# LayerNorm's normalization moved from VectorE to ScalarE in a three-part transformer stack

## The reference

```
def _layernorm(x, axis=-1, eps=1e-05):
    m = jnp.mean(x, axis=axis, keepdims=True)
    v = jnp.var(x, axis=axis, keepdims=True)
    return (x - m) / jnp.sqrt(v + eps)
...
    x = x + 0.5 * _L0_ffn_ref(_layernorm(x, axis=-1), ...)
    x = x + _L0_attn_ref(_layernorm(x, axis=-1), ...)
    x = x + 0.5 * _L0_ffn_ref(_layernorm(x, axis=-1), ...)
    x = x + 0.5 * _L1_ffn_ref(_layernorm(x, axis=-1), ...)
    x = x + _L1_attn_ref(_layernorm(x, axis=-1), ...)
    x = x + 0.5 * _L1_ffn_ref(_layernorm(x, axis=-1), ...)
```

## Time and profile before

| | |
|---|---|
| time, median of 3 runs | 4531.28 us (4527.89 to 4532.78) |
| the profiled execution | 4530.06 us |
| its span, first to last instruction | 4528.2 us |
| PE busy | 3917.3 us (87%) |
| DVE busy | 3219.1 us (71%) |
| ACT busy | 2058.9 us (45%) |
| POOL busy | 1146.4 us (25%) |
| L203, the normalization, 192 instructions | 80.1 us of DVE |
| L214, the power, 48 instructions | 48.5 us of POOL |
| L235, the copy of the transposes, 48 instructions | 28.7 us of ACT |

### The profile page before, as it was taken

One profiled execution on the slowest core, in us unless ns is written; L12 is line 12 of the kernel. 1 busy time (PEld: TensorE's weight loads), 2 busy tenths in 40 slices (PEclk: granted clock), 3 DMA queues, 4 the chain that ended last, 5 costly groups with the idle time before them and its releaser, 6 DMA issues. The chain is left out here.

```text
span 4528.2 us, 64140 instructions
## 1 busy us (share of the span) xinstructions
PE 3917.3 (87%) x23153; PEld 1796.6 (40%) x23153; DVE 3219.1 (71%) x6998; ACT 2058.9 (45%) x3088; POOL 1146.4 (25%) x943
## 2 busy tenths in 40 slices
PE   4799999968888849999999697758999999999865
PEld 2122222254444422222222544743444444444465
DVE  7799999926666678999997367665555555555565
ACT  3377777731145324777776311423333333333343
POOL 3000000000132130000000001753444444444465
PEclk9799999979999978999999798878999999999978
DMA  3111111120120031111111201430000000000144
GB/s 94 46 40 41 40 43 40 42 95 1 33 68 1 3 89 31 43 40 43 41 43 37 92 1 44 140 99 1 2 2 2 2 2 2 2 2 2 29 133 117
DMA packets 322709, 183.97 MB, mean 41 GB/s; under 512 B 169960, under 2 KB 282908, under 8 KB 322268
## 3 DMA queue, kind: packets, MB, share of 16 engines
q1 hardware_dynamic: 306044, 145.23, 11.8%
q0 software_dynamic: 14624, 34.37, 2.8%
q10 hardware_dynamic: 1728, 0.28, 0.0%
HBM read 109.91 MB, written 68.68 MB: 39 GB/s over the span
## 5 line engine op out<-in xcount | busy, mean ns | idle before, releaser
L646 DVE TENSOR_REDUCE ra_mh<-PS 128x1 f32<-128x512 f32 x2144 | 1341.9, 681 | 144.7 <-PE PS L524 135.8
L601 ACT ACTIVATE ra_p<-PS 128x1024 f32<-128x1024 f32 x1040 | 1011.8, 1021 | 482.3 <-PE PS L531 473.9
L524 PE MATMUL PS<-ra_k,ra_q 96*128 96x512 bf16 x2144 | 750.8, 392 | 2.3 <-DVE ra_mh L646 2.2
L540 PE MATMUL PS<-ra_p,ra_va 128*32 128x512 f32 x4192 | 569.2, 607 | 63.2 <-ACT ra_va L594 62.9
L531 PE MATMUL PS<-ra_q,ra_k 99*128 99x512 bf16 x2080 | 622.2, 380 | 1.7
L2081 ACT ACTIVATE ca_p<-PS 128x1024 f32<-128x1024 f32 (+3 forms) x384 | 310.8, 809 | 587.5 <-PE PS L2011 383.4
L2150 DVE TENSOR_REDUCE ca_mh<-PS 128x1 f32<-128x512 f32 (+3 forms) x768 | 388.1, 552 | 152.9 <-PE PS L1971 123.8
L500 POOL DMA_DIRECT2D o_heads<-ra_ot x134 | 70.3, 529 | 1649.3 <-ACT ra_ot L607 1649.3
L2116 POOL TENSOR_TENSOR ca_s<-ca_s,ca_p 128x1024 f32<-128x1024 f32 (+3 forms) x256 | 414.0, 1617 | 234.9 <-ACT ca_p L2081 229.6
L524 PEld LDWEIGHTS PS<-ra_k,ra_q 96*128 96x128 bf16 x2144 | 202.0, 97 | 659.8 <-DVE ra_mh L646 500.3
L2002 PE MATMUL PS<-ca_q,ca_k 64*128 64x512 f32 (+3 forms) x1536 | 344.4, 524 | 0.0
(11 more groups left out here) (270 smaller groups left out, 5616.8 us busy)
## 6 DMA issues: line engine op xcount, KB each, us to landing
ra_k<-qk_parts SPq DMA_DIRECT2D x136, 144.0 KB
ra_q<-qk_parts SPq DMA_DIRECT2D x408, 48.0 KB
o_heads<-ra_ot POOLq DMA_DIRECT2D x134, 128.0 KB, 3.4
ao_ot<-o_heads SPq DMA_DIRECT2D x16, 1024.0 KB
f_xg<-expert_tokens SPq DMA_DIRECT2D x56, 256.0 KB, 4.0
expert_outputs<-f_yb SPq DMA_DIRECT2D x56, 256.0 KB
qk_parts<-rp_parts SPq DMA_DIRECT2D x96, 128.0 KB, 2.4
expert_tokens<-X SPq DMA_DIRECT2D x28, 256.0 KB
```

What stands on the lines that cost most here:

```text
L524: pe.matmul(PS[:, 5 + place % 3, :], Q[0:KMAX, u, j, t * P:(t + 1) * P], K[0:KMAX, u, j, h * BT:(h + 1) * BT], start=True, stop=True).then ...
L540: mm = pe.matmul(PS[VW * j:VW * (j + 1), 4, :], VA[:, ub, step % KT, j, :], PR[:, s % 2, j, :], start=(s % KT == 0) if start is None else ...
L601: act.activation(PR[:, s % 2, PH * pair:PH * (pair + 1), :], PS[:, PH * pair:PH * (pair + 1), :], ACT.Exp, scale=float(DH) ** -0.5).then_i ...
L646: dve.tensor_reduce(mh[:, pair, c // HALVES, c % HALVES:c % HALVES + 1], PS[:, bank, :], AX.X, ALU.max).then_inc(s_max, 1)
```

## The change

The four normalizing instructions of each block go to ScalarE, as `activation` with the function Identity, a scale column (`ln_rs`) and a bias column (`ln_nb`, minus the mean times `ln_rs`), both per partition. GpSimd makes the bias column with two more small `tensor_tensor`: zero minus mean ahead of the power, and the product behind it. The signal `rstd` of a block now comes from that product. Normalizing a block is followed in ScalarE's stream by the copy of the block before. VectorE keeps the statistics; it may overwrite a buffer of `ln_mv` only when the block that used it is normalized, so it waits for that.

```
         dve.memset(self.eps[:, :], LN_EPS)
+        dve.memset(self.zero[:, :], 0.0)
         stats(0, 0)
         for it in range(NBLK // 2):
             for u in range(2):
                 n = 2 * it + u
+                if n:
+                    dve.wait_ge(self.normed, TPB * n)
                 stats(n + 1, 1 - u)
-                dve.wait_ge(self.rstd, n + 1)
-                for j in range(TPB):
-                    dve.tensor_scalar(self.XN[:, TPB * n + j, :], X[:, TPB * n + j, :], mv[:, u, j, 0:1],
-                                      self.rs[:, u, j:j + 1], ALU.subtract, ALU.mult).then_inc(self.normed, 1)
...
-                pool.wait_ge(self.vareps, n + 1)
+                pool.wait_ge(self.vareps, 3 * n + 1)
                 pool.wait_ge(self.normed, TPB * n)
-                pool.tensor_tensor(self.rs[:, u, :], self.ve[:, u, :], self.PW[:, :], ALU.pow).then_inc(self.rstd, 1)
+                pool.tensor_tensor(self.nm[:, u, :], self.zero[:, :], self.mv[:, u, :, 0], ALU.subtract).then_inc(self.vareps, 1)
+                pool.tensor_tensor(self.rs[:, u, :], self.ve[:, u, :], self.PW[:, :], ALU.pow).then_inc(self.vareps, 1)
+                pool.wait_ge(self.vareps, 3 * n + 3)
+                pool.tensor_tensor(self.nb[:, u, :], self.nm[:, u, :], self.rs[:, u, :], ALU.mult).then_inc(self.rstd, 1)
...
+    def turn(self, act, n):
+        act.wait_ge(self.turned, n + 1)
+        act.activation(self.XNT[:, BT * n:BT * (n + 1)], self.PS[:, n % 2, :], ACT.Copy).then_inc(self.copied, 1)
+
     def scalar(self, act):
-        for it in range(NBLK // 2):
-            for u in range(2):
-                n = 2 * it + u
-                act.wait_ge(self.turned, n + 1)
-                act.activation(self.XNT[:, bass.ds(BT * n, BT)], self.PS[:, u, :], ACT.Copy).then_inc(self.copied, 1)
+        for n in range(NBLK):
+            u = n % 2
+            act.wait_ge(self.rstd, n + 1)
+            for j in range(TPB):
+                act.activation(self.XN[:, TPB * n + j, :], self.X[:, TPB * n + j, :], ACT.Identity,
+                               bias=self.nb[:, u, j:j + 1], scale=self.rs[:, u, j:j + 1]).then_inc(self.normed, 1)
+            if n:
+                self.turn(act, n - 1)
+        self.turn(act, NBLK - 1)
         act.wait_ge(self.copied, self.COPIES)
```

More of the change, by code:

```diff
@@ L177, in __init__ @@
         self.mark = sb("ln_mark", [P, 1])
+        self.zero = sb("ln_zero", [P, TPB])
+        self.nm = sb("ln_nm", [P, 2, TPB])
+        self.nb = sb("ln_nb", [P, 2, TPB])
         self.stats_done, self.meanvar, self.vareps, self.rstd, self.normed, self.turned, self.copied = (
```

## The result

The changed kernel takes 4559.98 us (median of 4 runs, 4559.03 to 4561.03). The kernel before took 4530.75 beside it (4 runs, 4527.89 to 4532.78). The ratio is 1.0066, 95% interval 1.0054 to 1.0078: slower by 0.7%. The forecast was 4553, with a range of 4540 to 4564.

The account below looks back on a forecast made before the run. The prediction took each LayerNorm loop to be bound by a chain of latencies between two engines. Ropes -6.0, linear_attention +7.3, causal +6.7 and both ffn1 +15.1 made +23.1 us on 4530.06: 4553, range 4540 to 4564, its own 4548 to 4558.

Parts of the forecast that it names:

- The block B on ScalarE: Four normalizing instructions of a block on ScalarE: 1.42 us, 473 ns each, pitch near 0.32, against VectorE's 1.13.
- dearer: Rival, ScalarE's pointer columns cost more: block 1.64 us, turn 3.31, sum +33.1 us, 4563; chance 0.17.
- GpSimd's chain: From a block's normalization to the next block's start, through minus mean, power and product: 1.67 us, against 1.19.
- The plain LayerNorm: Basic LayerNorm loop in linear_attention and causal: first block 0.48, seven turns 5.39, last block 0.29, together 6.16 us longer.
- The circle before: LayerNorm loop before: GpSimd's power and VectorE's normalization alone set 2.32 us per block, VectorE idle in half of it.
- The holds: VectorE's next instruction delays GpSimd's last product: 1.1 us in linear_attention (L1308), 0.5 in causal (cast L2124).
- ffn1: Both ffn1 LayerNorms: first normalization waits behind ScalarE's router-weight copy; 7.6 and 7.5 us longer, 15.1 together.
- The ropes: rope_project, twice: projections 14.1 us behind the first memset instead of 23.0, which comes 5.9 later; net -3.0 each.
- The sum: Whole kernel: -6.0 + 7.3 + 6.7 + 15.1 = +23.1 us, giving 4553.
- Nearly free columns: Rival, ScalarE's pointer columns cost almost nothing: block 1.15 us, turn 2.82, sum +10.6 us, 4541; chance 0.15.
- Ropes give back everything: Rival, in rope_project L358 and L359 pass at L353's seam, 6.8 us more back each: +9.5, 4540; chance 0.07.
- Later work meets the constants: Rival, GpSimd's memsets hold VectorE's two-input work on the projections, L371 to L378: up to +7, 4560; chance 0.08.

Follow-up runs that it names:

- before_relaxed: Kernel before, with GpSimd's power waiting until the block before the last is normalized, not the last one; 4530.60 us, ratio 1.0000, turn 2.20 us.
- one_column: Changed kernel without the bias column in ScalarE's normalization, so the mean is not taken off; 4546.16 us, ratio 1.0034 to the kernel before, turn 2.89 us.
- relaxed: Changed kernel, GpSimd's power waiting for the block before the last, VectorE's statistics only for the bias column; 4509.13 us, ratio 0.9953 to the kernel before.
- no_column: Changed kernel without scale and bias columns in ScalarE's normalization, a plain copy of x; 4526.88 us in one run, turn 2.52 us.
- mean_early: Changed kernel with GpSimd making minus the mean ahead of its wait for the block before; 4555.00 us, ratio 1.0055 to the kernel before, turn 3.11 us.
- held_back: Changed kernel with VectorE's la_g build and mask cast waiting for GpSimd's last bias column; 4561.76 us in one run, LayerNorms 182.1 us.
- router_late: Changed kernel with ScalarE's two router-weight copies in ffn1 moved behind the second block's normalization; 4555.91 us, ratio 1.0058 to the kernel before.

## Why the prediction came out as it did

The mechanism was the forecast's: slower, by a longer loop between ScalarE and GpSimd in six LayerNorms, less what the ropes give back at the `memset`. The time (4559.98) fell inside 4540 to 4564, but above the forecast's own 4548 to 4558. The step that failed is one term.

- **The block B on ScalarE** was mis-sized: taken at 1.42, measured 1.65. The duration of one instruction (473) was right, 478. The pitch (near 0.32) was wrong, 0.391 on the mean of a block. It was built from L1620's 0.255, whose overlap of 0.131 doesn't hold for these instructions (0.087 by the same working). L1620 reads PSUM and computes another function, and whether either is the reason was not tried; L615, which reads PSUM too (128x1024), overlaps by 0.103 in the trace after, so reading PSUM alone doesn't settle it. The range for the second column, 1.24 to 1.51, was for that reason too low at both ends. This is the rival "dearer" (B = 1.64, chance 0.17, 4563), with the estimate from the Trainium skill's page ScalarE: Activation LUTs, section What ACT_TABLE_LOAD costs: 93 ns for each column, and about as much of overlap. The runs agree with both: 92 to 93 ns for a column and, start by start, 93 to 94 ns of overlap. A row of the same shape, but with another source and another function, was given more weight than a figure that fitted the case.
- **GpSimd's chain**, 1.67, came out at 1.61. The turn was 3.26, not 3.09: +0.94 a turn.
- **The plain LayerNorm**: with B = 1.65 the steps give 0.48 + 7 x 0.94 + 0.52 = 7.6 us instead of 6.16.
- **The circle before**: the prediction had GpSimd and VectorE's normalization alone in it and VectorE idle for half of the turn. VectorE's statistics (1.20) filled that gap, and the rows show it without idle time there; `before_relaxed`, with the circle opened, still took 2.20. The 2.32 was measured, so the sum isn't touched. It is why loosening the wait took only 0.12 us off a turn with VectorE.
- **The holds** were right in place and cause, 1.1 and 0.5 forecast, 0.91 and 0.35 measured. The cast in `causal` reads one SBUF tensor and held the product all the same, so a second input isn't needed for a hold. `linear_attention` grew by 8.77, against 7.6 + 0.9, and `causal` by 7.62, against 7.6 + 0.35. The two differences, +0.3 and -0.3, are the single turns with GpSimd's late start, one after and one before. Nobody forecast them, and that they cancel is luck.
- **`ffn1`**: the first normalization started behind the router's copy (2803.69), as forecast. The pair grew by 8.92 and 9.13 instead of 7.6 and 7.5. With the right B the step gives 7 x 3.26 + 1.65 against 23.05: 1.4 more, 9.0 and 8.9.
- **The ropes**: L367 held to the first seam, L372 to the end of the second `memset`, projections at 14.1 behind the first: all as forecast, to 0.01 us. The -3.0 became -1.85 (51.62 against 53.47), since the first `memset` comes 7.06 later with the longer turn, not 5.87. That is the first mistake again.
- **The sum** with B = 1.65 is -3.7 + 8.5 + 7.9 + 17.9 = +30.6. The table shows +30.7 for these parts, so close also because those two turns cancel; the time moved by 29.2.
- **The rivals.** Nearly free columns fell with `one_column`. "Ropes give back everything" fell: L372 was caught at the seam. "Later work meets the constants" fell too; VectorE with two SBUF inputs works beside a `memset` unheld, as this pair of the trace after shows (all 32 instructions of L385 lie between 684 and 693 ns, beside a `memset` or not):

```profile
58.48 1.80 POOL L358 MEMSET ra_q<- 64x2048 bf16 x1
59.30 1.29 DVE L385 TENSOR_TENSOR rp_qk<-rp_t 128x512 f32<-128x512 f32 x2
```

  The Trainium skill's rule in SBUF — State Buffer, section Who interferes with whom, cited in the prediction for the pair L1308 and L1290, has it so on its other half: a GpSimd instruction that only writes doesn't contend with it.

## What to carry to other kernels

Before an operation is moved to another engine, draw the circle that it stands in: what counts is the time from its input to its output on the new engine, with every small instruction put ahead of it, and not the busy time that the old engine sheds. If two engines wait for each other in turn, look first whether the wait between them is needed at all; here a buffer already allowed one block more. Loosening the waits was worth 51 us with ScalarE in the circle, and with VectorE, which was busy all the turn, nothing in the time. And a single instruction of 7 us in a line of 335 ns ones is a find by itself: it led to GpSimd's constants, whose later start gave 32 us without moving anything else.

## What was not expected of the hardware

- A pointer column on ScalarE costs its 93 ns in the pitch as well as in the duration, in both the first and the second column; back-to-back instructions overlapped by 93 to 94 ns for none, one and two columns, and by 87 on the mean of a block, whose first instruction takes 15 ns more.
- A normalization block and the copy behind it take 2.02 us in `relaxed`, though they are 1.65 and 0.59 by themselves: 24.17 lies 0.10 before the block's end (24.27), and 24.64 lies 0.12 before the copy's (24.76).
- ScalarE beside a `memset` was not slowed (1.65 at 37.49, 1.66 at 28.68 in `relaxed`), where VectorE's same work had taken 14.10. Of VectorE's instructions those with one SBUF input were held by a `memset` (L203, L353, L358), those with two (L385, 0.69 each) or with PSUM as input (L350, 0.41) were not.
- Two of GpSimd's small instructions start 0.15 us apart, though each is shown as 0.20, if the second doesn't need the first (19.74 and 19.89, 20.98 and 21.13); the product, which does, starts 0.08 behind the power's end.
- The stages' rest differs by some us between executions of equal code (1183.9 to 1186.9 for the first rope in after, `one_column`, `no_column`, `mean_early`, `held_back` and `router_late`). TensorE moves with it: in that stretch its same 5223 matmuls are busy for 1068.2 us in after, 1069.1 in `one_column`, 1069.3 in `no_column`, 1071.5 in `mean_early` and `held_back` and 1072.4 in `router_late`, while VectorE stays within 942.8 to 944.0 and ScalarE at 623.2. What makes the matmuls longer no run settles; the granted clock of the stretch reads 0.94 in all six.
